# Two edits to a fused state-space and mixture-of-experts kernel: fewer idle products on TensorE at the start, and a later place for one load in SyncE's list

## What is computed

```
mod = silu(c) @ wmod                       # six vectors per sequence
h = layernorm(x) * (1 + ca) + sa
xi = silu(h @ Win + bin)                   # 256 inner features
y[t] = C (decayed running sum of B xi) + Dp * xi[t]
x = x + ga * (y @ Wout + bout)
h = layernorm(x) * (1 + cb) + sb
p = softmax(h @ Wr + br); the best 2 of 8 experts, probabilities renormalised
expert e: layernorm(relu(layernorm(relu(h @ W1[e] + b1)) @ W2[e] + b2))
x = x + gb * (gate-weighted sum of the two experts' outputs)
```

## Time and profile before

| what | us |
|---|---|
| median of 3 runs | 518.74 |
| lowest and highest | 517.02, 518.94 |
| the profiled execution: its own time | 519.68 |
| the profiled execution: its span in the trace | 517.6 |

### The profile page before, as it was taken

One profiled execution on the slowest core, in us unless ns is written; L12 is line 12 of the kernel. 1 busy time (PEld: TensorE's weight loads), 2 busy tenths in 40 slices (PEclk: granted clock), 3 DMA queues, 4 the chain that ended last, 5 costly groups with the idle time before them and its releaser, 6 DMA issues.

```text
span 517.6 us, 14784 instructions
## 1 busy us (share of the span) xinstructions
PE 493.6 (95%) x3101; PEld 393.0 (76%) x3101; DVE 441.0 (85%) x2217; ACT 420.0 (81%) x1148; POOL 365.3 (71%) x483
## 2 busy tenths in 40 slices
PE   7989999999986999999998899999999999999996
PEld 6446665655544799989897789999999989899962
DVE  5778999998887699888887799988989999889893
ACT  5669888978764678888886788899999889999883
POOL 1003666666767778888888878888888888888870
PEclk9999999999997899999999999999999999999999
DMA  6980111145111779867616885666577577667555
GB/s 167 310 233 16 48 47 48 43 134 111 52 46 53 146 166 178 186 200 187 156 52 152 191 224 145 188 198 188 156 200 195 157 193 206 153 184 213 163 164 162
DMA packets 79786, 77.78 MB, mean 150 GB/s; under 512 B 11150, under 2 KB 72745, under 8 KB 79702
## 3 DMA queue, kind: packets, MB, share of 16 engines
q1 hardware_dynamic: 71286, 59.92, 47.4%
q0 software_dynamic: 8416, 16.93, 9.1%
HBM read 54.65 MB, written 22.59 MB: 149 GB/s over the span
## 4 chain that ended last, share of the span: by engine, by line
PE 42%; issue 8%; POOL 6%; DVE 1%; DMA 1%; POOLq 0%; ACT 0%; SPq 0%; DVEq 0%; ACTq 0%
PE bank L1673 15%; PE bank L1570 7%; PE bank L1563 4%; PE bank L1565 4%; PE bank L1564 4%; PE bank L1562 4%; POOL expert_rows L646 3%; PE bank L1554 2%; POOL xi L662 2%; POOL y L662 1%; PE bank L1507 1%; DMA hrow<-expert_rows 1%; PE bank L1686 1%; PE bank L1695 1%; POOL expert_results L674 0%
## 5 line engine op out<-in xcount | busy, mean ns | idle before, releaser
L646 POOL DMA_INDIRECT expert_rows<-rows_ring,slot x128 | 123.1, 962 | 96.1 <-issue 78.6
L674 POOL DMA_INDIRECT expert_results<-y,target x119 | 123.0, 1033 | 31.2 <-issue 26.7
L1673 PE MATMUL bank<-W,h2T 128*128 x720 | 95.5, 276 | 0.8 <-ACT h2T L773 0.3
L1673 PEld LDWEIGHTS bank<-W,h2T 128*128 128x128 f32 x720 | 87.7, 192 | 9.2 <-issue 1.6
L870 ACT ACTIVATE v<-wmod 128x128 f32<-128x128 f32 x135 | 41.9, 311 | 42.3 <-DVE vg L1373 39.2
L1362 DVE SCALAR_TENSOR_TENSOR wmod<-bank,rse,shifts 128x128 f32<-128x128 f32 x119 | 41.6, 350 | 32.9 <-PE bank L1673 25.0
L1562 PE MATMUL bank<-b_parts,onesr 128*128 x135 | 65.1, 482 | 0.7 <-DVE h3lo L1140 0.7
L758 ACT ACTIVATE n<-X,nm,rs 128x128 f32<-128x128 f32 x128 | 54.1, 485 | 8.1 <-DVE nm L1307 8.1
L1145 DVE BATCH_NORM_STATS2 stf<-h1T 128x6 f32<-128x512 f32 x90 | 59.3, 659 | 0.0
L1563 PE MATMUL bank<-W1hi,h3hi 128*128 x135 | 54.1, 401 | 0.0
L1570 PE MATMUL bank<-ident_wr,h1T 128*128 128x128 f32 x360 | 54.0, 273 | 0.0
(11 more groups left out here) (250 smaller groups left out, 1245.7 us busy)
## 6 DMA issues: line engine op xcount, KB each, us to landing
shifts<-expert_shifts SPq DMA_DIRECT2D x119, 192.0 KB, 4.2
hrow<-expert_rows SPq DMA_DIRECT2D x135, 65.0 KB
xi<-expert_results SPq DMA_DIRECT2D x12, 512.0 KB, 6.0
out_x<-X SPq DMA_DIRECT2D x15, 256.0 KB
X<-in_L_attn_x SPq DMA_DIRECT2D x7, 512.0 KB, 7.4
W1lo<-in_L_ffn_W SPq DMA_DIRECT2D x4, 512.0 KB, 6.8
expert_rows<-rows_ring,slot POOLq DMA_INDIRECT x128
expert_results<-y,target POOLq DMA_INDIRECT x119
```

Of the source, the lines that this page charges most:

```text
L646: nc.gpsimd.indirect_dma_start(out=rows_d, out_offset=bass.IndirectOffsetOnAxis(ap=slot[q][:, n // TOPK, n % TOPK:n % TOPK + 1], axis=0), ...
L674: nc.gpsimd.indirect_dma_start(out=results_d, out_offset=bass.IndirectOffsetOnAxis(ap=target[i % TARGETS][:], axis=0), in_=y[k], in_offset ...
L1673: ins = mm(acc, rT[(s - 4) % DEPTH][:, ch * P:(ch + 1) * P], W2[:, bass.ds(e4 * CF + ch, 1), :], start=(ch == 0), stop=(ch == CF - 1))
```

## The change

The first group of idle products has five instead of six. The second group, between the modulation vectors and the turning of `cp`, goes. In SyncE's list the request for batch 0 stands behind tile 57 instead of tile 54; `piece_tile` and all that ACT, DVE and POOL do with it stay as they are, and so do the requests of all other batches.

```diff
-            LOADED_AT = {piece_tile(b, 0) + 1: b for b in range(EARLY)}
+            LOADED_AT = {piece_tile(b, 0) + (4 if b == 0 else 1): b for b in range(EARLY)}
...
-            keep_busy(6)
+            keep_busy(5)
             pe.wait_ge(dve_setup, SETUP_CT)
             pe.wait_ge(mod_loaded, 16)
             for n in range(5):
                 mm(bank[4][:, n * B:(n + 1) * B], wmod[:, n * D:(n + 1) * D], cT[:], start=True, stop=True)
             mm(bank[4][0:B, D:2 * D], cT[:], wmod[:, 5 * D:6 * D], start=True, stop=True).then_inc(pe_setup, 1)
-            keep_busy(6)
             pe.wait_ge(small_loaded, 16 * 7)
```

## The result

| | us |
|---|---|
| kernel before, median of 12 runs | 517.56 |
| changed kernel, median of 12 runs | 521.29 (519.60 to 522.22) |
| ratio, with its 95% interval | 1.0054 (1.0038 to 1.0071) |
| profiled executions: span before, span of the changed kernel | 517.6, 518.0 |

The changed kernel is slower by 0.54%, 2.8 us by the ratio. The forecast was +2.5 us.

A forecast was written before the change was run, and what follows sets the result against it. POOL bounds the kernel up to about 280 us, then, after one late load of expert rows, TensorE. From the 518.74 us median, 2.0 us gained at the start and 4.5 us lost give 521.2 us, range 517.8 to 523.4 us.

The forecast's parts named there:

- The bound behind tile 55: TensorE from about 300 us: no hole until 480 us, so whatever holds it up there is paid in full.
- Part two, the wait: Around tile 57: the later request makes ACT wait for the load and delays `hidden(55)` on TensorE; 2.6 us lost.
- Part two, the clock: TensorE behind its idle stretch near 300 us: granted clock falls to 0.50, costing 1.9 us, between 1.7 and 2.75.
- the first rival: Around tile 57: the load stalls ACT, but the clock holds; +0.6 us, 519.4 us; chance 0.22.
- Part one, the start: Kernel start: without the second idle group the first large products start 2.7 us earlier, partly at half speed; 2.0 us gained.
- The third rival: Kernel start: clock rises 4 us later, so the start gains nothing; 523.2 us; chance 0.15 together with another rival.
- part two: Moved request around tile 57: ACT's wait and the fallen clock together lose 4.5 us, ends 2.4 and 6.0 us.

The follow-up runs named there:

- start_alone: The changed kernel's idle products with the request for batch 0 left behind tile 54, as in the kernel before; 516.89 us, ratio 0.9981 to the kernel before.
- request_alone: The kernel before with only the request for batch 0 moved behind tile 57, all idle products kept; 523.45 us, ratio 1.0108 to the kernel before.
- start_at56: The changed kernel with the request for batch 0 behind tile 56 instead of 57; 517.23 us, ratio 0.9987 to the kernel before.
- no_idle: The changed kernel also without the first idle group and the three idle products of step -1; 522.75 us, ratio 1.0082 to the kernel before.
- filled_wait: The changed kernel with 17 idle products on TensorE ahead of the hidden values of tile 55; 520.22 us, ratio 1.0038 to the kernel before.
- start_at55: The changed kernel with the request for batch 0 behind tile 55 instead of 57; 515.29 us, ratio 0.9955 to the kernel before.

## Why the prediction was right

**The bound behind tile 55.** Right: no hole of TensorE up to 480 us, and the 4.7 us lost by 302.84 us are the 4.7 us between the spans of `start_alone` and the changed kernel.

**Part two, the wait.** Right in place and size. `request_alone` is the profile to hold against the forecast's times, since it starts as the kernel before did. The request stood at 296.16 us (forecast 295.75), ACT read at 301.61 us (301.35 to 302.25), `hidden(55)` began at 302.91 us (302.4 to 303.3), and TensorE was idle for 3.40 us (3.1). In the changed kernel ACT was idle for 5.76 us (4 to 6; 6.38 in the second profile) and TensorE for 4.07 us, which is longer than forecast, and 3.1 us were lost at `hidden(55)`, where I took 2.6. Two small misses cancel in this: the load took 5.3 us to land and not 5.6 to 6.5, and from L845 to `hidden(55)` it was 298.87 - 297.56 = 1.31 us and not 1.1.

**Part two, the clock.** Right: it fell, for 3.4 us, at 1.6 us, where I took 1.9 between 1.7 and 2.75. Together 4.7 us against 4.5. That an idle stretch of 2.01 us in `start_at56` left the clock alone shows why the first rival, the stall without the fall, was a real one. The argument against that rival was weaker than it looked: it compared lengths of idle stretches with the 2.84 us of the earlier trace rows. That stretch began at 158.32 - 2.84 = 155.48 us, and the kernel before shows:

```profile
155.00:156.00 1.00, 0.48 (x9) 0.24 (x7) 0.98 (x5) 1.00 (x3) 0.69 (x2) 1.00 0.01 0
156.00:157.00 1.00, 0.00 (x0) 0.00 (x0) 0.90 (x8) 0.09 (x1) 0.73 (x1) 0.80 0.20 67
```

A mean of 0.80 is 0.4 us at the low level, so the clock was down from about 156.6 us, 1.1 us into the idle stretch. TensorE had stood idle for 1.94 us shortly before as well, ahead of 153.51 us. So this case says nothing of how long a single stretch must be.

**Part one, the start.** The mechanism was right for the profile at hand, where POOL's first store moved by 46.43 - 43.95 = 2.48 us, and the term was mis-sized: "I take 2.0, between 1.35 and 2.7". `start_alone` measured 0.2 to 1.8 us. The bounds came from one execution of the kernel before, in which the clock rose at about 13 us, and I varied that moment only for the changed kernel's products. The kernel before hangs on it too. Where the clock rises early, its second idle group costs 1.60 us instead of 2.93 us, the modulation vectors ahead of it are made 0.8 us sooner, and its first large product starts as early as the changed kernel's. The third rival had the clock rise at another time, but later, and in the changed kernel alone; that it may rise earlier in the kernel before stood nowhere. Nor did the rise stay near 13 us in the changed kernel: its large products are fast from about 12.7 us in the first profile and from about 14.7 us in the second.

**Why the sum came out.** +4.7 and -1.4 give +3.3 us; the ratio gives +2.8, from +2.0 to +3.7. The single edits' ratios give -1.0 + 5.6 = +4.6 us, with intervals wide enough to hold this. The forecast of +2.5 lies only 0.3 us from the ratio's +2.8, and that is closer than its terms deserve: the start was taken 0.6 to 1.0 us too large and part two 0.2 us too small by the profiles, so some of this closeness is luck. The first profiles show only +0.4 us, since that of the kernel before had a late start (46.43 us, matched only by `request_alone`), and POOL's stretch behind it was 1.3 us longer too: from POOL's first store to the addition for tile 43 it is 294.71 - 46.43 = 248.3 us, in the changed kernel 290.90 - 43.95 = 246.95 us:

```profile
290.90 0.49 POOL L662 TENSOR_TENSOR y<-wmod,shifts 128x128 f32<-128x128 f32 x1
```

What makes POOL's stretch vary was not tried.

## What to carry to other kernels

A request that is moved back in a queue for the sake of what stands behind it must be checked against its own reader: time of the new place, plus the landing, minus the time of the first use. Here the slack was some 0.6 us (a request 1.4 us later cost ACT 0.8 us), so each tile further back stopped ACT and all that stands behind it in ACT's order. One tile was nearly free, and it already took away the wait for rows at step 53 that moving by three tiles was meant to remove. And a term that rests on when the clock rises has to be read in several executions, of both kernels, before it gets a size.

## What the runs showed of the hardware

The moment at which TensorE's clock rises after the same work differs from one profile to the next. In four profiles of one kernel the idle group at 8 to 9 us ran at the fast pace once (1.60 us) and at the slow pace for nearly all of its length three times (2.84, 2.87 and 2.93 us), and the first large product began at 11.55, 13.60, 13.62 and 14.24 us. The four don't come from one chip.

In the middle, around 300 us, TensorE's idle stretches of 3.40, 3.48, 4.07 and 4.72 us (`request_alone`, `no_idle`, the changed kernel twice) were each followed by some 3.4 us at the low level, at a price of 1.6 us. The one of 2.01 us in `start_at56` was not, nor was that of 0.75 us in `filled_wait`. Around 156 us, where TensorE worked in short pieces, the clock was down 1.1 us into an idle stretch.

The same 512 KB load took differing times from request to the first read by ACT where ACT stood waiting for it: 4.81 us in `start_at56`, 5.05 in `start_at55`, 5.38 in the changed kernel and 6.03 in `filled_wait`.
